# Re-ordering the attention phase of a four-layer fp32 transformer kernel on TensorE, and splitting a low part between two engines

## The chip, the cores and the metric
The kernel runs on one core of one Trainium2 chip. The metric is the device time of one execution in microseconds (us). TensorE is PE in the profile (PEld is its weight load), VectorE is DVE, ScalarE is ACT, GpSimd is POOL, SyncE is SP.

## The reference
Sixteen sequences of 256 tokens by 256 features go through four transformer layers, each conditioned by a vector per sequence. In every layer:

```
h = norm(x) * (1 + sc1) + sh1
x = x + gate1 * (softmax(q k^T / 4) v) @ Wo        # 16 heads of 16; layer 1 causal, layer 3 rotates q and k
h = norm(x) * (1 + sc2) + sh2
x = x + gate2 * act(h @ W1 + b1) @ W2              # W1: 256 -> 1024, gelu; layer 3: 256 -> 2048, a * silu(b)
```

All data are fp32. Layer 0 shares keys between heads (the weights are repeated, so the work is the same), layer 1 is causal, layer 3 has rotary positions, a root-mean-square norm and the gated hidden layer.

## The kernel before
**Tiles and steps.** A tile is one sequence in one layer, so there are 64. The work is a software pipeline over steps t: in a step, tile t+1 (`s.q`) gets its first norm and its queries, keys and values, tile t (`s.a`) its scores, softmax and outputs, tile t-1 (`s.r`) its output projection and second norm, and tile t-2 (`s.m`) its hidden layer (`up` and `down`, eight each). Eleven steps of each layer (44 in all) run in a hardware loop; the others are written out. In a loop, semaphores are compared with values held in registers. All five queues (PE, ACT, DVE, POOL, SP) are written out by hand in one order each, and wait for each other by semaphores. That order is what the change edits.

**Split products.** A product of two fp32 matrices is made of fp32r parts, a high part and a low part (value minus high part): high by high, low by high, high by low. `H2[0]` and `H2[1]` are the two parts of the second norm's result, the input of the `up` products. `project` issues six products of 256 columns per 128 outputs.

**The attention phase.** Scores are computed twice. First in the normal layout, from which DVE takes row maxima (`maximum`); then transposed with the maxima subtracted (`transposed_pair(p)`, L713, two heads in two halves of 64 rows), from which ACT takes the exponentials (L885) into a ring `PR` of 8 heads. `outputs(g)` (L738) multiplies four heads of `PR` by V in columns of 32. In front of the exponential of head h, ACT waits for `pe_pv` of outputs group h//4 - 2, which frees the ring:

```
at_least(ac, pe_pv, 4 * a_ + h // 4 - 1)
```

A transposed pair waits until the heads that used its PSUM banks four heads earlier are exponentiated. The first lines of each step's end on PE are: queries, pairs 0 and 1, maxima, keys, pairs 2 and 3, values half 0, outputs 0, pairs 4 and 5, outputs 1, second norm (`norm_2`, L592, four transposes), pairs 6 and 7, outputs 2, values half 1, outputs 3. In the causal layer each pair is followed by two mask products (L507).

**Second norm.** PE transposes TOK into a bank; DVE (`modulate_2`) writes HF (L1089, twice) and its high part H2h (L1095); POOL then writes the low part H2l (L1271). The next step begins on PE with `up(0)`, `up(1)`, which need both parts, then `outputs_to_tokens` (L602), `up(2)`, `down(0)`. `up(2)` writes the bank of `up(0)` and so waits for the activation of `up(0)` (`ac_g`, L861; in layer 3 `dv_g`, L966).

Of the kernel before, what the change touches and what calls it, by code (L numbers as in the profile page):

```python
# [21 lines left out]
F32 = mybir.dt.float32  # L22
# [52 lines left out]
NORM2_BANK = (0, 7)  # L75
# [9 lines left out]
def build(nc, a, out):  # L85
    ctx = ExitStack()
    with ctx:
# [52 lines left out]
        def bank(n, parts=2):  # L140
# [15 lines left out]
        dv_max, dv_rz, dv_on, dv_ot, dv_wo, dv_dn, dv_gh, dv_g, dv_swap, dv_rot, dv_rot2, dv_v, dv_o, dv_f2 = (  # L156
            sem("dv_" + x) for x in ("max", "rz", "on", "ot", "wo", "dn", "gh", "g", "swap", "rot", "rot2", "v", "o", "f2"))
# [321 lines left out]
        def _(pe):  # L479
# [23 lines left out]
            def body(s):  # L503
# [45 lines left out]

                def up(j):  # L550

                    m, dst = s.m, bank(3 - j % 2)
                    if j == 0:
                        weights(s.lm, "1", s.sm, *((0, 4, 2, 6) if s.lm == ROPE else (0, 2)))
                        pe.wait_ge(dv_h2, m + 1)
                        pe.wait_ge(po_h2, m + 1)
                        key_read(s)
                    elif j == 1:
                        at_least(pe, dv_v, s.nq)
                    elif s.lm == ROPE:  # L560
                        pe.wait_ge(dv_g, NJ * (m - NSEQ * ROPE) + j - 1)
                    else:
                        pe.wait_ge(ac_g, NJ * m + j - 1)
                    if j == NJ // 2:
                        weights(s.lm, "1", s.sm, *((1, 5, 3, 7) if s.lm == ROPE else (1, 3)))
                    last = project(dst[:, 0, :], cols(W1, j * P), H2)
                    if s.lm == ROPE:
                        last = project(dst[:, 1, :], cols(W1, DFF + j * P), H2)
                    last.then_inc(pe_up, 1)
# [57 lines left out]
                def norm_2():  # L627

                    if s.a is not None:
                        pe.wait_ge(ac_exp, H * s.a + last_user(ST_BANKS[rope][0:HB] + (NORM2_BANK[rope],), HB) + 1)  # L630
                    pe.wait_ge(dv_xn2, s.r + 1)
                    to_features(bank(NORM2_BANK[rope]), TOK).then_inc(pe_h2, 1)

# [88 lines left out]
                def outputs(g):  # L722
# [6 lines left out]
                    if g == 2:  # L729
                        at_least(pe, dv_dn, s.m_done)  # L730
                        if rope and s.r is not None:
                            pe.wait_ge(dv_f2, s.r + 1)
# [24 lines left out]
                up_if(0, 1)  # L757
# [39 lines left out]
                if scored:  # L797
                    transposed_pair(2)
                    transposed_pair(3)
                    values(0)  # L800
                    outputs(0)
                    transposed_pair(4)
                    transposed_pair(5)
                    outputs(1)
                    if s.r is not None:
                        norm_2()
                    transposed_pair(6)
                    transposed_pair(7)
                    outputs(2)
                    values(1)  # L810
# [10 lines left out]
        def _(ac):  # L821
# [84 lines left out]
            def modulate_1(s):  # L906
# [3 lines left out]
                at_least(ac, dv_h2, s.nr)  # L910
# [11 lines left out]
        def _(dv):  # L922
# [22 lines left out]
            def body(s):  # L945
# [136 lines left out]
                def modulate_2():  # L1082
# [12 lines left out]
                    nc.vector.tensor_copy(H2[0][:], HF[:]).then_inc(dv_h2, 1)  # L1095

# [17 lines left out]
                if s.lq == ROPE:  # L1114
# [7 lines left out]
                    rotate(s, pe_k, 3, GK, V_BK, V_BKR, 1)  # L1122
                    modulate_2()
                    evacuate(0)
                    values_out()
# [3 lines left out]
                else:  # L1129
                    split_q()  # L1130
                    split_k()
                    normalise_2()
                    modulate_2()
                    evacuate(0)
                    values_out()
# [60 lines left out]
        def _(po):  # L1196
# [40 lines left out]
            def body(s):  # L1237
# [30 lines left out]
                if s.r is not None:  # L1268
                    po.wait_ge(dv_f2, s.r + 1)
                    po.wait_ge(dv_h2, s.r + 1)  # L1270
                    nc.gpsimd.tensor_tensor(H2[1][:], HF[:], H2[0][:].bitcast(F32), ALU.subtract).then_inc(po_h2, 1)  # L1271
# [174 lines left out]
```

## Time and profile before

| | us |
|---|---|
| median of 3 runs | 2283.18 (2279.66 to 2284.66) |
| the profiled execution's own time | 2276.1 |
| its span in the trace | 2274.3 |
| PE busy | 2175.1 (96% of the span) |
| DVE busy | 1701.4 |
| ACT busy | 1252.4 |
| POOL busy | 1087.9 |

A line of the page's groups or of the timeline gives the source line, the engine, the operation, what it writes and reads, and how often. Matmuls are pipelined: one of 256 columns has a duration of 0.28 us, while the next starts 0.12 us after it, so starts are to be compared, not durations.

### The profile page before, as it was taken

To read this page: it belongs to the slowest core of one execution; us is meant where nothing else is said; L and a number is where in the kernel's file an instruction comes from. 1 tells how busy PE (TensorE), PEld (TensorE's weight loads), DVE (VectorE), ACT (ScalarE), POOL (GpSimd) and SP (SyncE) were. 2 spreads that over 40 slices of the span, in tenths; PEclk is the share of its full clock that TensorE was granted. 3 is DMA by queue.
4 is the path that set the end of the run, shared out by engine and by line. 5 is a ranking of instruction groups with operands and counts; after the bars stand their busy time and mean duration, and the time that the engine had idled before them with its cause. 6 is when DMAs were issued, how large, how long until landed. Compare 5 with 4: busy or idle time off the path is not lost.

```text
span 2274.3 us, 63435 instructions
## 1 busy us (share of the span) xinstructions
PE 2175.1 (96%) x20136; PEld 1824.5 (80%) x20136; DVE 1701.4 (75%) x4378; ACT 1252.4 (55%) x2620; POOL 1087.9 (48%) x1333
## 2 busy tenths in 40 slices
PE   5699999999999999999999999999999999999997
PEld 4578888888888888888878888888787878787877
DVE  3567777777777766776787777777888888888873
ACT  1366666666665555555676666666645444535341
POOL 1244554445544544454555444455554445444444
PEclk7699999999999999999999999999999999999998
DMA  6221222222221122112232222212221111111210
GB/s 230 89 72 64 63 69 70 71 64 77 89 91 63 58 70 72 60 59 92 90 99 64 70 74 65 63 63 80 83 78 66 59 63 60 62 64 58 68 58 15
DMA packets 164960, 166.12 MB, mean 73 GB/s; under 512 B 29328, under 2 KB 144400, under 8 KB 164848
## 3 DMA queue, kind: packets, MB, share of 16 engines
q1 hardware_dynamic: 164848, 164.69, 22.5%
q8 instruction: 63, 1.03, 0.2%
q14 instruction: 49, 0.40, 0.1%
HBM read 58.47 MB, written 4.39 MB: 28 GB/s over the span
## 4 chain that ended last, share of the span: by engine, by line
PE 86%; DVE 6%; issue 2%; SPq 1%; ACT 1%; POOL 1%; DMA 1%; POOLq 0%; ACTq 0%; DVEq 0%
PE B L483 36%; PE B L583 14%; PE B L738 10%; PE B L713 8%; PE B L530 7%; PE B L592 4%; PE B L602 2%; PE B L507 2%; DVE NEGM L959 2%; PE B L686 2%; SPq L1346 1%; ACT PR L885 1%; DVE G L966 0%; ACT G L855 0%; POOL GHl L1241 0%
## 5 line engine op out<-in xcount | busy, mean ns | idle before, releaser
L885 ACT ACTIVATE PR<-B 128x512 f32<-128x512 f32 (+1 forms) x1024 | 505.2, 570 | 277.2 <-PE B L713 186.6
L1241 POOL TENSOR_TENSOR GHl<-G,GHh 128x256 fp32r<-128x256 f32 x512 | 377.8, 738 | 472.7 <-ACT GHh L861 286.7
L959 DVE TENSOR_REDUCE NEGM<-B 128x2 f32<-128x512 f32 x768 | 484.6, 681 | 93.1 <-PE B L530 93.0
L483 PE MATMUL B<-H2h,W1h 128*128 128x256 f32 x1280 | 397.1, 310 | 3.1 <-issue 3.1
L483 PE MATMUL B<-H2h,W1l 128*128 128x256 f32 x1280 | 362.7, 283 | 0.0
L483 PE MATMUL B<-H2l,W1h 128*128 128x256 f32 x1280 | 362.1, 283 | 0.0
L861 ACT ACTIVATE G<-B,VEC 128x256 f32<-128x256 f32 x384 | 182.3, 475 | 291.7 <-PE B L483 291.7
L583 PE MATMUL B<-W2h,GHh 128*128 128x256 f32 x1024 | 296.4, 289 | 1.7 <-POOL GHl L1241 1.7
L583 PE MATMUL B<-W2l,GHh 128*128 128x256 f32 x1024 | 289.6, 283 | 0.0
L583 PE MATMUL B<-W2h,GHl 128*128 128x256 f32 x1024 | 288.9, 282 | 0.0
L483 PEld LDWEIGHTS B<-H2h,W1h 128*128 128x128 f32 x1280 | 243.8, 190 | 44.1 <-issue 26.0
L738 PE MATMUL B<-PR,V 128*32 128x256 f32 (+1 forms) x4096 | 262.6, 374 | 14.1 <-ACT PR L885 8.8
L1271 POOL TENSOR_TENSOR H2l<-HF,H2h 128x512 fp32r<-128x512 f32 x64 | 82.1, 1283 | 340.0 <-DVE H2h L1095 340.0
L483 PEld LDWEIGHTS B<-H2l,W1h 128*128 128x128 f32 x1280 | 244.8, 191 | 0.0
L483 PEld LDWEIGHTS B<-H2h,W1l 128*128 128x128 f32 x1280 | 243.9, 191 | 0.0
L713 PE MATMUL B<-QS,KS 64*128 64x256 f32 (+1 forms) x2048 | 226.2, 313 | 10.6 <-ACT PR L885 1.7
L713 PEld LDWEIGHTS B<-QS,KS 64*128 64x128 f32 x2048 | 151.1, 187 | 93.0 <-ACT PR L885 48.0
L530 PE MATMUL B<-KS,QS 48*128 48x256 f32 (+1 forms) x2048 | 199.1, 311 | 19.3 <-DMA KS<-KHL 11.7
L583 PEld LDWEIGHTS B<-W2h,GHh 128*128 128x128 f32 x1024 | 194.9, 190 | 10.4 <-DVE GHh L971 2.1
L956 DVE CUSTOM_DVE_ANT_0 B<-B,MASK 128x128 f32<-128x128 f32 (+1 forms) x512 | 165.6, 388 | 39.9 <-PE B L530 39.9
L583 PEld LDWEIGHTS B<-W2l,GHh 128*128 128x128 f32 x1024 | 195.3, 191 | 0.0
L583 PEld LDWEIGHTS B<-W2h,GHl 128*128 128x128 f32 x1024 | 195.3, 191 | 0.0
(149 smaller groups left out, 4737.4 us busy)
## 6 DMA issues: line engine op xcount, KB each, us to landing
QS<-QHL SPq DMA_DIRECT2D x768, 64.0 KB, 2.1
KS<-KHL SPq DMA_DIRECT2D x768, 64.0 KB, 2.1
GA<-gate_scratch SPq DMA_DIRECT2D x48, 256.0 KB, 3.2
GM<-gate_scratch SPq DMA_DIRECT2D x48, 256.0 KB, 3.4
RAW<-in_w SPq DMA_DIRECT2D x36, 256.0 KB, 3.2
CW<-in_cw SPq DMA_DIRECT2D x3, 1536.0 KB, 13.5
X<-in_x SPq DMA_DIRECT2D x2, 2048.0 KB, 10.3
QS<-MT SPq DMA_DIRECT2D x256, 4.0 KB
```

The lines of the kernel that those rows point to most:

```text
L483: last = nc.tensor.matmul(dst, w[i], x[j], start=(first_k and n == 0), stop=(last_k and n == 2))
L530: last = nc.tensor.matmul(bank(banks[h])[:, i, 0:keys], QS[b:b + STK, p, i * P:(i + 1) * P], KS[b:b + STK, p, 0:keys], start=True, stop=True)
L583: last = nc.tensor.matmul(bank(7)[:, i, :], GH[x][:, j % RING, i * P:(i + 1) * P], W2[y][:, j, :], start=(j == 0 and n == 0 and i == 0), s ...
L592: last = nc.tensor.transpose(dst[:, f, i * P:(i + 1) * P], src[:, i, f * P:(f + 1) * P], IDENT[:])
L713: last = nc.tensor.matmul(B[:, banks[h], k * T:k * T + T - first], KS[b:b + ROWS, p, k * P:(k + 1) * P], QS[b:b + ROWS, p, first:T], start ...
L738: last = nc.tensor.matmul(bank(6 + g // 2)[32 * j:32 * j + 32, g % 2, c], V[:, k, HV * h:HV * h + 32], PR[:, h % PRING, k, 0:n], start=(k ...
L861: last = nc.scalar.activation(dst[:, j % RING, :], bank(3 - j % 2)[:, 0, :], ACT.Gelu, bias=VEC[:, s.lm, V_B1 + j:V_B1 + j + 1])
L885: nc.scalar.activation(PR[:, h % PRING].rearrange("p k q -> p (k q)")[:, 0:n], src[:, 0:n], ACT.Exp, scale=SCALE).then_inc(ac_exp, 1)
L956: last = nc.vector.tensor_tensor_reduce(src[:, i, 0:keys], src[:, i, 0:keys], unmasked, -1.0, HIGHEST, ALU.add, ALU.min, NEGM[:, i, c:c + 1])
L959: last = nc.vector.tensor_reduce(NEGM[:, :, c], src, op=ALU.max, axis=AX.X, negate=True)
L1241: nc.gpsimd.tensor_tensor(GH[1][:, j % RING, :], G[:, j % RING, :], GH[0][:, j % RING, :].bitcast(F32), ALU.subtract).then_inc(po_gl, 1)
L1271: nc.gpsimd.tensor_tensor(H2[1][:], HF[:], H2[0][:].bitcast(F32), ALU.subtract).then_inc(po_h2, 1)
```

## The change
Seven edits, in the code's order:

- The bank of the second norm's transposes becomes 3 in layer 3 (it was 7); elsewhere it stays bank 0. `norm_2` there waits for the rotation of the keys, and `outputs(2)` no longer waits for `dv_f2`.
- The PE order of the attention phase: values half 0 comes in front of pairs 2 and 3, values half 1 in front of pairs 4 and 5, outputs 0 and 1 behind pairs 4 and 5, `norm_2` behind pairs 6 and 7 (in layer 3 behind outputs 2 as well).
- `up(0)` and `up(1)` become `first_ups`: first the products that read H2's high part for both, then those that read its low part for both.
- H2's low part is halved: DVE subtracts feature half 0 (`dv_h2lo`), POOL half 1.
- DVE evacuates the values (`values_out`) in front of `modulate_2`.

```diff
-NORM2_BANK = (0, 7)
+NORM2_BANK = (0, 3)
...
+                def first_ups():
+
+                    m = s.m
+                    weights(s.lm, "1", s.sm, *((0, 4, 2, 6) if s.lm == ROPE else (0, 2)))
+                    pe.wait_ge(dv_h2, m + 1)
+                    halves = [(0, 0), (1, DFF)] if s.lm == ROPE else [(0, 0)]
+                    for low in range(2):
+                        for j in range(2):
+                            dst = bank(3 - j)
+                            if low and j == 0:
+                                pe.wait_ge(dv_h2lo, m + 1)
+                                pe.wait_ge(po_h2, m + 1)
+                            elif j == 0:
+                                key_read(s)
+                            elif not low:
+                                at_least(pe, dv_v, s.nq)
+                            for half, c in halves:
+                                w = cols(W1, c + j * P)
+                                terms = [(0, k) for k in range(KD)] if low else [(i, k) for k in range(KD) for i in range(2)]
+                                for n, (i, k) in enumerate(terms):
+                                    last = nc.tensor.matmul(dst[:, half, :], w[i][:, k], H2[low][:, k],
+                                                            start=(n == 0 and not low and half == 0), stop=(n == KD - 1 and low == 1),
+                                                            skip_group_check=True)
+                            if low:
+                                last.then_inc(pe_up, 1)
...
                 def norm_2():
 
-                    if s.a is not None:
-                        pe.wait_ge(ac_exp, H * s.a + last_user(ST_BANKS[rope][0:HB] + (NORM2_BANK[rope],), HB) + 1)
+                    if rope:
+                        pe.wait_ge(dv_rot, 2 * (s.q - NSEQ * ROPE) + 2)
+                    elif s.a is not None:
+                        pe.wait_ge(ac_exp, H * s.a + last_user(ST_BANKS[0][0:HB] + (NORM2_BANK[0],), HB) + 1)
...
                     if g == 2:
                         at_least(pe, dv_dn, s.m_done)
-                        if rope and s.r is not None:
-                            pe.wait_ge(dv_f2, s.r + 1)
...
-                up_if(0, 1)
+                if s.m is not None:
+                    first_ups()
...
                 if scored:
+                    values(0)
                     transposed_pair(2)
                     transposed_pair(3)
-                    values(0)
-                    outputs(0)
+                    values(1)
                     transposed_pair(4)
                     transposed_pair(5)
+                    outputs(0)
                     outputs(1)
+                    transposed_pair(6)
+                    transposed_pair(7)
+                    if rope:
+                        outputs(2)
                     if s.r is not None:
                         norm_2()
-                    transposed_pair(6)
-                    transposed_pair(7)
-                    outputs(2)
-                    values(1)
+                    if not rope:
+                        outputs(2)
                     outputs(3)
...
                     nc.vector.tensor_copy(H2[0][:], HF[:]).then_inc(dv_h2, 1)
+                    dv.wait_ge(dv_h2, s.r + 1)
+                    nc.vector.tensor_tensor(H2[1][:, 0], HF[:, 0], H2[0][:, 0].bitcast(F32), ALU.subtract).then_inc(dv_h2lo, 1)
...
-                    nc.gpsimd.tensor_tensor(H2[1][:], HF[:], H2[0][:].bitcast(F32), ALU.subtract).then_inc(po_h2, 1)
+                    nc.gpsimd.tensor_tensor(H2[1][:, 1], HF[:, 1], H2[0][:, 1].bitcast(F32), ALU.subtract).then_inc(po_h2, 1)
```

## Rows read from the trace of the kernel before

**Rows 1.** Windows, a step each: us, busy PE, PEld, DVE, ACT, POOL; clock, DMA

```profile
1449.33:1480.97 31.64, 31.39 (x300) 26.17 (x296) 24.14 (x51) 20.30 (x43) 15.85 (x19) 1.00 0.22 67
1032.36:1064.89 32.53, 32.53 (x316) 27.19 (x312) 23.40 (x95) 19.32 (x45) 17.73 (x21) 1.00 0.27 86
1872.97:1911.55 38.58, 37.36 (x349) 32.05 (x345) 33.29 (x76) 17.52 (x34) 18.18 (x24) 1.00 0.20 62
```

**Rows 2.** Timeline of PE, layer 2, end of a step and start of the next

```profile
1469.32 0.74 PE L713 MATMUL B<-QS,KS 64*128 64x256 f32 x8
...
1471.86 1.13 PE L713 MATMUL B<-QS,KS 64*128 64x256 f32 x8
...
1473.81 1.07 PE L738 MATMUL B<-PR,V 128*32 128x256 f32 x16
1474.82 0.74 PE L713 MATMUL B<-QS,KS 64*128 64x256 f32 x8
...
1476.49 0.66 PE L592 MATMUL B<-IDENT,TOK 128*128 128x128 f32 x4
...
1477.64 0.50 PE L713 MATMUL B<-QS,KS 64*128 64x256 f32 x4
...
1479.08 0.38 PE L483 MATMUL B<-WQ0h,H1h 128*128 128x256 f32 x1
...
1479.97 1.07 PE L738 MATMUL B<-PR,V 128*32 128x256 f32 x16
1480.97 0.39 PE L483 MATMUL B<-H2h,W1h 128*128 128x256 f32 x1
...
1482.52 1.03 PE L602 MATMUL B<-IDENT,OR 128*128 128x128 f32 x8
1483.31 0.36 PE L483 MATMUL B<-H2h,W1h 128*128 128x256 f32 x1
```

**Rows 3.** Timeline of ACT over the same stretch of layer 2

```profile
1472.39 2.07 ACT L885 ACTIVATE PR<-B 128x512 f32<-128x512 f32 x4
...
1475.43 2.07 ACT L885 ACTIVATE PR<-B 128x512 f32<-128x512 f32 x4 [0.97 <-PE B L713]
...
1482.20 0.47 ACT L861 ACTIVATE G<-B,VEC 128x256 f32<-128x256 f32 x1 [0.94 <-PE B L483]
1482.57 0.47 ACT L861 ACTIVATE GHh<-B,VEC 128x256 fp32r<-128x256 f32 x1
```

**Rows 4.** Timeline of DVE over the same stretch of layer 2

```profile
1477.42 1.00 DVE L1089 TENSOR_SCALAR HF<-B,COND 128x256 f32<-128x256 f32 x2 [2.33 <-PE B L592]
1478.54 0.43 DVE L1095 CAST H2h<-HF 128x512 fp32r<-128x512 f32 x1
```

**Rows 5.** The page's costliest groups, the low part of the hidden layer

```profile
L1241 POOL TENSOR_TENSOR GHl<-G,GHh 128x256 fp32r<-128x256 f32 x512 | 377.8, 738 | 472.7 <-ACT GHh L861 286.7
```

**Rows 6.** One line's instructions (L258): ns min/median/max, first and last start

```profile
L258 DVE TENSOR_TENSOR W1l<-RAW,W1h x16: 659/682/1440, 55.8 to 1686.9; 128x512 fp32r<-128x512 f32 x16
```

**Rows 7.** Timeline of PE, causal layer 1

```profile
1055.36 0.44 PE L713 MATMUL B<-QS,KS 64*128 64x256 f32 x4
...
1057.47 0.86 PE L738 MATMUL B<-PR,V 128*32 128x256 f32 x16
...
1061.72 0.45 PE L713 MATMUL B<-QS,KS 64*128 64x256 f32 x4
```

**Rows 8.** Timeline of ACT, causal layer 1

```profile
1058.95 1.64 ACT L885 ACTIVATE PR<-B 128x384 f32<-128x384 f32 x4 [1.25 <-PE B L507]
...
1065.92 0.47 ACT L861 ACTIVATE G<-B,VEC 128x256 f32<-128x256 f32 x1 [1.04 <-PE B L483]
```

**Rows 9.** Timeline of PE, layer 3

```profile
1860.62 0.74 PE L713 MATMUL B<-QS,KS 64*128 64x256 f32 x8
...
1870.07 1.07 PE L738 MATMUL B<-PR,V 128*32 128x256 f32 x16 [0.71 <-ACT PR L885]
```

**Rows 10.** Timeline of DVE, layer 3

```profile
1875.37 0.48 DVE L966 SCALAR_TENSOR_TENSOR G<-B,VEC,G 128x256 f32<-128x256 f32 x1 [0.51 <-ACT G L855]
```

More of the change, by code:

```diff
@@ L155, in build @@
             sem("dv_" + x) for x in ("st1", "mv1", "xn1", "st2", "mv2", "xn2", "h1", "h2", "qh", "q", "kh", "k"))
-        dv_max, dv_rz, dv_on, dv_ot, dv_wo, dv_dn, dv_gh, dv_g, dv_swap, dv_rot, dv_rot2, dv_v, dv_o, dv_f2 = (
-            sem("dv_" + x) for x in ("max", "rz", "on", "ot", "wo", "dn", "gh", "g", "swap", "rot", "rot2", "v", "o", "f2"))
+        dv_max, dv_rz, dv_on, dv_ot, dv_wo, dv_dn, dv_gh, dv_g, dv_swap, dv_rot, dv_rot2, dv_v, dv_o, dv_f2, dv_h2lo = (
+            sem("dv_" + x) for x in ("max", "rz", "on", "ot", "wo", "dn", "gh", "g", "swap", "rot", "rot2", "v", "o", "f2", "h2lo"))
         po_t1, po_rs1, po_t2, po_rs2, po_h1, po_h2, po_gl, po_xb1, po_x1, po_xb2, po_x2, po_v, po_w, po_init, po_rot = (
@@ L548, in key_read @@
                         at_least(pe, dv_k, s.nq)
+                def first_ups():
[22 more added lines that the diff above has]
+                                last.then_inc(pe_up, 1)
                 def up(j):
                     m, dst = s.m, bank(3 - j % 2)
[L553 to L560, printed above, removed]
+                    if s.lm == ROPE:
                         pe.wait_ge(dv_g, NJ * (m - NSEQ * ROPE) + j - 1)
@@ L909, in modulate_1 @@
                     return
-                at_least(ac, dv_h2, s.nr)
+                at_least(ac, dv_h2lo, s.nr)
                 at_least(ac, po_h2, s.nr)
@@ L1122, in body @@
                     rotate(s, pe_k, 3, GK, V_BK, V_BKR, 1)
+                    values_out()
                     modulate_2()
                     evacuate(0)
-                    values_out()
                     evacuate(1)
@@ L1132, in body @@
                     normalise_2()
+                    values_out()
                     modulate_2()
                     evacuate(0)
-                    values_out()
                     evacuate(1)
```

## The prediction, on record before the run
> **What bounds the kernel now.** I read the windows first, one step each. PE is busy nearly all of a step (31.39 of 31.64 us in layer 2, 32.53 of 32.53 in the causal layer, 37.36 of 38.58 in layer 3) at full granted clock, and DVE, ACT and POOL are far from it [rows 1]. So a step is the sum of PE's starts, plus PE's waits. Durations overlap, therefore I read the timeline of PE by starts [rows 2]. Twelve first up products take 1482.52 - 1480.97 = 1.55 us: 12 x 0.12, and 0.10 to get going. Six V products between runs of other tile shapes take 1479.97 - 1479.08 = 0.89, against 6 x 0.12 = 0.72. Each change of shape (128 rows, pairs in 64 rows, outputs in 32 columns) thus costs about 0.17 to 0.18 us. The waits: the run of pairs 2 and 3 takes 1.13 where that of pairs 4 and 5 takes 0.74, and pair 7 starts only at 1477.64 [rows 2], 0.14 after ACT's group of exponentials 8 to 11 ends (1475.43 + 2.07 = 1477.50) [rows 3]. ACT's chain of exponentials therefore already touches PE's path. In layer 3 outputs 2 wait 0.71 at 1870.07 [rows 9].
>
> **What is removed.** In a layer without masks the new order has 10 shape changes from the queries to the next up where the old has 13: 3 x 0.17 = about 0.5 us a step. The wait of 0.39 in pairs 2 and 3 has half 0 of V as cover. In layer 3 the wait of 0.71 in outputs 2 loses its reason. The number of products is unchanged everywhere, so at PE alone I would book a gain of about 0.9 us a step, before new waits.
>
> The Trainium skill ("TensorEngine Tiling (Array Packing)", Key Properties) says that a change of tiling mode drains TensorE. By that, fewer changes are a gain; the 0.17 us agrees, and the sum needs nothing more from it.
>
> **What is added: the exponentials, layer 2 in a loop.** I schedule the new order by hand on the old clock, from the first pair at 1469.32, which nothing moves.
> - V half 0 comes ahead of pair 2, in the same shape as the keys before it: 6 x 0.12 = 0.71. Pair 2 goes from 1471.86 to 1472.57. ACT, idle by then, takes its exponential 4 at +0.61, the lag of pair 4 (1474.82) to exponential 8 (1475.43) [rows 2, 3]: 1473.18, where before it was at 1472.39.
> - Four exponentials take 2.07, spaced 0.49, 0.59 for one alone [rows 3]. Pair 4 needs heads 4 and 5: 1473.18 + 0.49 + 0.59 + 0.14 = 1474.41. Outputs 0 follow two pairs (0.67) later, at 1475.08, and end 1.07 later at 1476.15.
> - Exponential 8 overwrites the ring slot that outputs 0 read. Before, outputs 0 were over at 1474.88 and it went at 1475.43. Now it waits until about 1476.22: +0.79. Behind it in ACT's queue stand only exponentials and the table load (15 ends at 1480.2, in time for outputs 3 at 1480.33). Exponentials 8 to 11 end at 1478.29, pair 7 starts at 1478.43 instead of 1477.64.
> - Behind pair 7 (0.43) come the transposes at 1478.86. From their start to the end of H2h were 1478.97 - 1476.49 = 2.48 [rows 2, 4], and 0.14 to PE: 2.62. The high part is there for PE at 1481.48. Transposes and outputs 2 and 3 alone need 0.58 + 1.85 (1.01 each [rows 2] less the shape change between them) and are over at 1481.29. So the next step begins at 1481.48 instead of 1480.97: **+0.51**. The cover that H2h had (pairs 6 and 7, a half of V) is what the move took away.
>
> **What is added: the first ups.** `up(0)` now ends with the tenth product instead of the sixth: 4 x 0.12 = 0.48 later. Its activation ended 1482.57 + 0.47 - 1480.97 = 2.07 behind the step's start [rows 3, 2], with 0.14 it lets `up(2)` go at 2.21, and `up(2)` went at 2.34: 0.13 of room. So +0.35. What becomes late behind it is `down(0)`, whose low part follows the same activation; it moves along with `up(2)`.
>
> To it comes the halved low part. DVE's half starts 0.1 behind H2h and takes about 0.45 (an estimate: 256 columns, a little under the 0.48 of [rows 10]); POOL's takes 0.74 [rows 5]. If both run at once, POOL's half is there for PE 0.15 + 0.74 + 0.14 = 1.03 behind H2h, and the ninth product, the first to read it, is due at 0.14 + 0.10 + 8 x 0.12 = 1.20: hidden. If POOL has to wait for DVE, it is there at 0.1 + 0.45 + 0.03 + 0.74 + 0.14 = 1.46: 0.2 of stall. The trace has subtractions on DVE with two SBUF inputs that take 682 ns at the median and up to 1440 [rows 6], so such an instruction can be held up for as long as it runs. I take 0.2, and 0 as the lower bound. Together **+0.55**.
>
> The Trainium skill ("SBUF — State Buffer", Who interferes with whom) says that a DVE instruction with two SBUF inputs and a GpSimd instruction that reads SBUF exclude each other. By that the 0.2 is right; without it the sum would be 47 x 0.2 = about 9 us lower. The 1440 ns above agrees.
>
> `outputs_to_tokens` waits for DVE's two evacuations, which now come behind one more instruction; they end about 0.1 ahead of or behind its turn, inside the 0.55. POOL's copy of V, SP's loads of the stacks (released by pairs 3 and 7) and the moved `values_out` have more than 1 us until their readers, so I cost them at nothing.
>
> **The other steps.** Layer 0 has layer 2's order, so 22 loop steps: 22 x 1.06 = 23.3.
> - Causal, 11 loop steps, the same chain [rows 7, 8]: pair 2 at 1055.36 + 0.71 = 1056.07; pair, mask, pair, mask and V in 2.11, pair 4 at 1058.18; outputs 0 after two pairs with masks (1.40) at 1059.58 (before: 1057.47), over at 1060.44; exponential 8 at 1060.50 instead of 1058.95; number 11 over at 1062.14; pair 7 at 1062.28 instead of 1061.72; transposes 0.52 later; + 2.62 = 1065.42, where the window ends at 1064.89. +0.53, and +0.55: 11 x 1.08 = 11.9.
> - Layer 3, 11 loop steps, counted from pair 0 (1860.62 [rows 9]): exponential 4 at 3.86; pair 5 needs exponential 6, so 3.86 + 0.98 + 0.60 + 0.14 = 5.58; outputs 0 at 5.91, over at 6.98; exponential 11 over at 9.12; pair 7 at 9.27; outputs 2 at 9.70, transposes at 10.70, H2h for PE at 13.32, that is 1873.94 against 1872.97 [rows 1]: +0.97. The removed wait of 0.71 is thus paid back by one for H2h. `up(0)` has 24 - 4 = 20 products in front of its end instead of 12, 0.96 more; DVE's product ended at 1875.85 [rows 10], + 0.96 + 0.14 = 1876.95 against `up(2)` at 1872.97 + 24 x 0.12 + 0.10 + 0.79 = 1876.74: +0.2. 11 x 1.17 = 12.9.
> - The 19 scored steps outside the loops compare with constants: there the first activation comes 1065.92 - 1064.89 = 1.03 behind the step's start [rows 8, 1], not 1.23. With 0.2 off at each of two places I take 0.7: 13.3.
>
> Sum: 23.3 + 11.9 + 12.9 + 13.3 = 61 us on the profiled execution's 2276.1, so 2337. The median of the runs lies 7.1 above that execution: 2344.
>
> **The rivals.**
> - Forecast, slower by 32 to 80 us: the chain outputs 0, exponential 8, pair 7, transposes, H2h sets the step. Lower bound: no stall in the low part (-9), and waits in series shorter by 0.3 us a step than I read them (-19), so +32. Upper: each wait in a loop 0.3 longer, since `key_read` and others are now tested behind the wait for H2h: +80. Chance 0.84.
> - The exponentials hold PE back, but H2h doesn't, and the first ups cost only their 0.35 or less. Then a step is at +0.32 (1481.29 against 1480.97) + 0.15 to 0.35: 63 x 0.4 = +25, 2308. For it: PE and H2h differ by only 0.19 in layer 2. Against it: 0.97 in layer 3. Chance 0.06.
> - Faster: PE is the only bound. This needs exponential 8 not to wait on outputs 0, that is, outputs 0 over before 1475.43 + 0.3. Then -0.9 a step stays, +0.35 for the first ups: 62 x -0.55 = -34, 2249. For it: 96% busy. Against it: the code's wait, and a PE that is already held at pair 7. It decides when pair 4 starts before 1474.0. Chance 0.06.
> - No change: gain and waits cancel. It needs -0.5 us a step against my chain on both sides. 2283 within 4.6. Chance 0.04.
>
> **How the numbers follow.** Within 0.2% (4.6 us, what a measurement can tell) is the last rival; slower are the first two. The range 2308 to 2366 takes in the forecast's bounds (2315 and 2363) and the second rival's time. Slower 0.90, same 0.04, faster 0.06.
>
> **What would show it.** Layer 2's step at 32.7 instead of 31.64, layer 3's near 39.7, the causal one near 33.6; exponential 8 released by outputs 0 (L738), not by a pair; idle PE in front of pairs 6 and 7 and in front of the first up, released by H2h on DVE; ahead of `up(2)` a wait on ACT's activation; POOL's half of H2l starting behind DVE's. If pair 7 follows pair 6 without a gap, or PE finds H2h ready, I am wrong.

## The result, and the profile after

The changed kernel takes 2332.09 us (median of 4 runs, 2329.48 to 2337.9) against 2281.45 us for the kernel before (median of 4, 2279.66 to 2284.66): 1.0228 times as long, with a 95% interval of 1.0211 to 1.0244. The forecast was 2344 in a range of 2308 to 2366. The profiled execution took 2329.48 us against the 2276.1 on which the sum was made: +53.4, where the sum said +61. Runs of one kernel differ by up to 9 us, and some 6 of them can lie ahead of the first layer: of 96 products in the set-up (L360, the same in both), the last starts at 34.2 in the trace of the kernel before, where one takes 263 ns, and at 40.4 in that of experiment 10, where one takes 374.

The page of the changed kernel: the line of busy engines, the line of the chain that ended last, and one group of the costliest.

```profile
PE 2170.3 (93%) x20136; PEld 1833.4 (79%) x20136; DVE 1719.0 (74%) x4442; ACT 1249.2 (54%) x2620; POOL 1059.1 (46%) x1333
...
PE 81%; DVE 6%; ACT 4%; issue 4%; SPq 1%; DMA 1%; POOL 1%; ACTq 0%; DVEq 0%; POOLq 0%
...
L1266 POOL TENSOR_TENSOR GHl<-G,GHh 128x256 fp32r<-128x256 f32 x512 | 377.6, 738 | 458.9 <-ACT GHh L884 280.4
```

ACT's share of the chain was 1% in the kernel before, and PE's 86%. PE has as many products as before and is less busy in time, so all of the loss is idle PE. One step each of layer 2, of the causal layer 1 and of layer 3, windows of the changed kernel (columns as in [rows 1]):

```profile
1518.34:1550.95 32.61, 31.41 (x297) 26.35 (x297) 24.36 (x53) 20.24 (x43) 15.38 (x19) 1.00 0.20 65
889.18:922.79 33.61, 32.65 (x312) 27.56 (x313) 23.78 (x96) 18.47 (x43) 15.35 (x19) 1.00 0.20 63
1918.46:1957.96 39.50, 37.26 (x345) 32.07 (x345) 33.56 (x78) 17.38 (x34) 17.72 (x24) 1.00 0.18 60
```

Against [rows 1] the steps are 0.97, 1.08 and 0.92 us longer at the same granted clock of 1.00, and PE, which had 0.00 to 1.22 us of idle time in a step, has 0.96 to 2.24. The engines that got more to do (DVE in every layer) stay below the step's length (33.56 of 39.50 for DVE in layer 3 at most).

Timeline of PE in the changed kernel, layer 2, from the first pair of a step through the first ups of the next:

```profile
1538.85 0.74 PE L734 MATMUL B<-QS,KS 64*128 64x256 f32 x8
...
1542.08 0.74 PE L734 MATMUL B<-QS,KS 64*128 64x256 f32 x8
...
1543.86 0.76 PE L734 MATMUL B<-QS,KS 64*128 64x256 f32 x8
1544.55 1.93 PE L757 MATMUL B<-PR,V 128*32 128x256 f32 x32
1546.92 0.50 PE L734 MATMUL B<-QS,KS 64*128 64x256 f32 x4 [0.43 <-ACT PR L908]
1547.90 0.50 PE L734 MATMUL B<-QS,KS 64*128 64x256 f32 x4 [0.48 <-ACT PR L908]
1548.33 0.66 PE L611 MATMUL B<-IDENT,TOK 128*128 128x128 f32 x4
1548.92 1.93 PE L757 MATMUL B<-PR,V 128*32 128x256 f32 x32
1550.95 0.38 PE L570 MATMUL B<-H2h,W1h 128*128 128x256 f32 x1
...
1552.01 0.71 PE L570 MATMUL B<-H2l,W1h 128*128 128x256 f32 x4
1552.56 1.06 PE L621 MATMUL B<-IDENT,OR 128*128 128x128 f32 x8
1553.62 0.39 PE L483 MATMUL B<-H2h,W1h 128*128 128x256 f32 x1
...
1554.54 0.36 PE L602 MATMUL B<-W2h,GHh 128*128 128x256 f32 x1
```

Timeline of ACT over the same stretch:

```profile
1542.62 2.07 ACT L908 ACTIVATE PR<-B 128x512 f32<-128x512 f32 x4 [0.76 <-PE B L734]
1545.69 4.03 ACT L908 ACTIVATE PR<-B 128x512 f32<-128x512 f32 x8 [0.99 <-PE B L757]
...
1553.10 0.47 ACT L884 ACTIVATE GHh<-B,VEC 128x256 fp32r<-128x256 f32 x1
```

The line to see is ACT's second one. In [rows 3] the exponentials 8 to 11 waited for a pair (`<-PE B L713`). Here number 8 waits for outputs 0 (`<-PE B L757`), which are the first half of PE's row x32 at 1544.55 and are over about 1.07 later. Counted from pair 0, exponential 8 starts at 6.84 (before: 1475.43 - 1469.32 = 6.11), and from there all is late. Pair 6 waits 0.43, pair 7 waits 0.48 and starts at 9.05 (before 8.32), the transposes of the second norm follow at 9.48, and the next step's first up comes at 12.10 where it came at 11.65: +0.45.

Timeline of PE in layer 3 of the changed kernel, the same stretch:

```profile
1944.81 0.74 PE L734 MATMUL B<-QS,KS 64*128 64x256 f32 x8
...
1954.01 0.50 PE L734 MATMUL B<-QS,KS 64*128 64x256 f32 x4 [0.48 <-ACT PR L908]
...
1955.44 0.66 PE L611 MATMUL B<-IDENT,TOK 128*128 128x128 f32 x4
1956.02 1.07 PE L757 MATMUL B<-PR,V 128*32 128x256 f32 x16
1957.96 0.38 PE L570 MATMUL B<-H2h,W1h 128*128 128x256 f32 x1 [0.86 <-DVE H2h L1118]
```

Here the transposes come last but for outputs 3, and PE stands idle for 0.86 us on the high part of the norm. That takes the place of the wait of 0.71 in [rows 9], which is gone.

The low part of the second norm, timelines of DVE and POOL in layer 2, and the page's view by line (ns min/median/max):

```profile
1549.27 0.99 DVE L1112 TENSOR_SCALAR HF<-B,COND 128x256 f32<-128x256 f32 x2 [4.05 <-PE B L611]
1550.39 0.43 DVE L1118 CAST H2h<-HF 128x512 fp32r<-128x512 f32 x1
1550.85 0.43 DVE L1120 TENSOR_TENSOR H2l<-HF,H2h 128x256 fp32r<-128x256 f32 x1
```
```profile
1550.97 0.90 POOL L1296 TENSOR_TENSOR H2l<-HF,H2h 128x256 fp32r<-128x256 f32 x1 [9.29 <-DVE H2h L1118]
...
1553.65 1.46 POOL L1266 TENSOR_TENSOR GHl<-G,GHh 128x256 fp32r<-128x256 f32 x2 [1.23 <-ACT GHh L884]
```
```profile
L1296 POOL TENSOR_TENSOR H2l<-HF,H2h x64: 894/906/919, 131.2 to 2301.4; 128x256 fp32r<-128x256 f32 x64
```
```profile
L1120 DVE TENSOR_TENSOR H2l<-HF,H2h x64: 424/426/429, 131.1 to 2301.3; 128x256 fp32r<-128x256 f32 x64
```

POOL's half takes 906 ns at the median (894 to 919 in all 64 steps), where the same operation on the same shape takes 738 elsewhere (L1266). DVE's takes 426 and begins 0.12 us earlier in this step.

**A step taken apart.** For the experiments a step is cut in two: from its first up to the queries ("first part") and from the queries to the next first up ("attention"). Both are differences of starts in PE's timeline, for one step inside each loop, in us (other steps in the middle of a loop differ from it by 0.04 or less):

```
              layer 0          causal           layer 2          layer 3
before        18.33 + 13.17    18.42 + 14.11    18.47 + 13.18    24.69 + 13.89
after         18.87 + 13.60    18.94 + 14.67    19.02 + 13.63    24.83 + 14.67
difference     0.54 +  0.43     0.52 +  0.56     0.55 +  0.45     0.14 +  0.78
```

### The profile page after: what moved, and what is told of

It is laid out like the page before. It is cut to its first block, busy times and chain, and to the rows that moved or that the text cites. A ratio compares the mean times of both kernels' runs of the same rounds, so it can differ in the third digit from the quotient of the medians.

```text
span 2327.7 us, 63529 instructions
## 1 busy us (share of the span) xinstructions
PE 2170.3 (93%) x20136; PEld 1833.4 (79%) x20136; DVE 1719.0 (74%) x4442; ACT 1249.2 (54%) x2620; POOL 1059.1 (46%) x1333
## 4 chain that ended last, share of the span: by engine, by line
PE 81%; DVE 6%; ACT 4%; issue 4%; SPq 1%; DMA 1%; POOL 1%; ACTq 0%; DVEq 0%; POOLq 0%
PE B L483 30%; PE B L602 15%; PE B L734 8%; PE B L530 7%; PE B L757 6%; PE B L570 6%; PE B L611 4%; ACT PR L908 4%; PE B L621 2%; PE B L507 2%; PE B L707 2%; DVE NEGM L982 2%; SPq L1371 1%; DVE HF L1112 1%; DVE H2h L1118 1%
## 5 line engine op out<-in xcount | busy, mean ns | idle before, releaser
L1266 POOL TENSOR_TENSOR GHl<-G,GHh 128x256 fp32r<-128x256 f32 x512 | 377.6, 738 | 458.9 <-ACT GHh L884 280.4
L483 PE MATMUL B<-H2h,W1h 128*128 128x256 f32 x960 | 300.7, 313 | 0.5 <-DVE G L989 0.2
L1296 POOL TENSOR_TENSOR H2l<-HF,H2h 128x256 fp32r<-128x256 f32 x64 | 57.9, 905 | 495.8 <-DVE H2h L1118 495.8
L734 PE MATMUL B<-QS,KS 64*128 64x256 f32 (+1 forms) x2048 | 218.3, 310 | 59.8 <-ACT PR L908 52.6
L483 PE MATMUL B<-H2h,W1l 128*128 128x256 f32 x960 | 271.6, 283 | 0.0
L483 PE MATMUL B<-H2l,W1h 128*128 128x256 f32 x960 | 271.2, 283 | 0.0
L1112 DVE TENSOR_SCALAR HF<-B,COND 128x256 f32<-128x256 f32 x128 | 63.7, 540 | 254.9 <-PE B L611 254.9
L757 PE MATMUL B<-PR,V 128*32 128x256 f32 (+1 forms) x4096 | 239.3, 371 | 0.4 <-ACT PR L908 0.4
L483 PEld LDWEIGHTS B<-H2h,W1h 128*128 128x128 f32 x960 | 182.0, 190 | 28.7 <-ACT GHh L884 8.0
L530 PEld LDWEIGHTS B<-KS,QS 48*128 48x128 f32 x2048 | 140.8, 187 | 63.8 <-issue 19.9
## 6 DMA issues: line engine op xcount, KB each, us to landing
X<-in_x SPq DMA_DIRECT2D x2, 2048.0 KB, 10.3
```

The lines of the kernel that those rows point to most:

```text
L483: last = nc.tensor.matmul(dst, w[i], x[j], start=(first_k and n == 0), stop=(last_k and n == 2))
L530: last = nc.tensor.matmul(bank(banks[h])[:, i, 0:keys], QS[b:b + STK, p, i * P:(i + 1) * P], KS[b:b + STK, p, 0:keys], start=True, stop=True)
L734: last = nc.tensor.matmul(B[:, banks[h], k * T:k * T + T - first], KS[b:b + ROWS, p, k * P:(k + 1) * P], QS[b:b + ROWS, p, first:T], start ...
L757: last = nc.tensor.matmul(bank(6 + g // 2)[32 * j:32 * j + 32, g % 2, c], V[:, k, HV * h:HV * h + 32], PR[:, h % PRING, k, 0:n], start=(k ...
L1266: nc.gpsimd.tensor_tensor(GH[1][:, j % RING, :], G[:, j % RING, :], GH[0][:, j % RING, :].bitcast(F32), ALU.subtract).then_inc(po_gl, 1)
```

## The experiments

Unless a ratio is said to be to something else, it is to the kernel before, run beside on the same chip, with its 95% interval.

**1. The first ups and the halved low part alone.** The kernel before, with `first_ups()` and both subtractions as in the change; order, banks and `values_out` stay as they were.

```diff
-                up_if(0, 1)
+                if s.m is not None:
+                    first_ups()
...
+                    dv.wait_ge(dv_h2, s.r + 1)
+                    nc.vector.tensor_tensor(H2[1][:, 0], HF[:, 0], H2[0][:, 0].bitcast(F32), ALU.subtract).then_inc(dv_h2lo, 1)
...
-                    nc.gpsimd.tensor_tensor(H2[1][:], HF[:], H2[0][:].bitcast(F32), ALU.subtract).then_inc(po_h2, 1)
+                    nc.gpsimd.tensor_tensor(H2[1][:, 1], HF[:, 1], H2[0][:, 1].bitcast(F32), ALU.subtract).then_inc(po_h2, 1)
```

> The kernel before with the low-part edits alone (first ups in two passes, low part halved between DVE and POOL); the order of the attention phase, the banks and values_out stay. Theory A (up(0) ends four products later, up(2) waits for its activation): a step in a loop of layers 0 to 2 is 0.35 us longer, one outside 0.15, one of layer 3 0.2; about +16 us in all, 2297. All of it between the step's start and up(2); the attention phase is unchanged. Rival B (the 0.54 us that the changed kernel loses there comes from the late high part and from POOL's half alone): here the parts are ready early, so within 5 us of the kernel before.

Measured: 2298.86 us, 1.0073 [1.0045, 1.0101]. The attention of layer 2 stays at 13.20, the first part grows from 18.47 to 18.92. So these edits reach only the first part, as the forecast's chain wants it, and cost 0.45 of the 0.55 us there, where 0.35 was expected.

**2. The order alone.** The kernel before with the new order, banks and place of `values_out`, but the old `up(0)` and `up(1)`, and the whole low part on POOL.

```diff
-NORM2_BANK = (0, 7)
+NORM2_BANK = (0, 3)
...
                 if scored:
+                    values(0)
                     transposed_pair(2)
                     transposed_pair(3)
-                    values(0)
-                    outputs(0)
+                    values(1)
                     transposed_pair(4)
                     transposed_pair(5)
+                    outputs(0)
                     outputs(1)
-                    if s.r is not None:
-                        norm_2()
                     transposed_pair(6)
                     transposed_pair(7)
...
+                        norm_2()
+                    if not rope:
+                        outputs(2)
                     outputs(3)
```

> The changed kernel with the old ups and the whole low part on POOL: the new order alone. Theory A (the high part of H2 is the last thing to come, and the low part 1.44 us behind it is hidden only by the two passes): the first up goes 1.44 us later than in the changed kernel, 0.54 us of it is won back before up(2); about +0.9 us a step in layers 0 to 2 and +1.3 in layer 3, 2395 us. Rival B (the exponentials alone hold PE back and the low part has cover): at or below the changed kernel's 2332, since the 0.54 us in the first ups goes away.

Measured: 2406.68 us, 1.0548 [1.0521, 1.0575]. Timelines of PE and of POOL, layer 2:

```profile
1472.43 0.38 PE L483 MATMUL B<-H2h,W1h 128*128 128x256 f32 x1 [1.62 <-POOL H2l L1274]
```
```profile
1470.93 1.26 POOL L1274 TENSOR_TENSOR H2l<-HF,H2h 128x512 fp32r<-128x512 f32 x1 [9.29 <-DVE H2h L1098]
```

With the late norm the old first ups wait for POOL's whole subtraction: 1470.93 + 1.26 + 0.14 = 1472.33, and the first of them starts at 1472.43. The time is 12 us above the 2395 expected. The attention takes 15.15 instead of 13.18. Two things follow. The new order alone is far worse than the change as a whole. And the edits of the low part, two passes and halving together, are a repair of it: with them the order costs 0.45 us in layer 2 instead of 1.97, and their own price of 0.55 is on top. How much of the repair each of the two gives in the new order, no run shows.

**3. Outputs 0 back ahead of pairs 4 and 5.** The changed kernel, one line moved.

```diff
                     values(1)
+                    outputs(0)
                     transposed_pair(4)
                     transposed_pair(5)
-                    outputs(0)
                     outputs(1)
```

> The changed kernel with outputs 0 moved back in front of pairs 4 and 5 (behind V half 1). Theory A (exponential 8 waits for the ring slot that outputs 0 read): exponential 8 is released by pair 4, about 0.45 us earlier, pair 7 and the high part of H2 as well, and a step is about 0.45 us shorter although it has one shape change more; about -27 us against the changed kernel, 2305. Rival C (V half 0 ahead of pair 2 delays all exponentials and is the whole cause) and rival D (the second norm's place): exponentials 8 to 15 come no earlier for PE, 2332 within 5 us.

Measured: 2300.97 us, 1.0090 [1.0064, 1.0117], so 31 us less than the changed kernel, and near experiment 1, which has the low-part edits and none of the order. Timeline of ACT, layer 2:

```profile
1399.65 4.03 ACT L908 ACTIVATE PR<-B 128x512 f32<-128x512 f32 x8 [0.59 <-PE B L734]
```

Exponential 8 is released by a pair again, 6.43 behind pair 0 (which starts at 1393.22), and the attention of layer 2 is back at 13.22, that of layer 3 at 14.05. The first part keeps its 19.00. This one line holds nearly the whole of what the order costs. That it does not fall below 13.18, although two shape changes fewer are made than before, is the rest of the lateness: both halves of V now stand in front of outputs 0, which start 4.82 behind pair 0 (1398.04 in PE's timeline) instead of 4.49.

**4. The norm back ahead of pairs 6 and 7.** The changed kernel, layers 0 to 2.

```diff
                     outputs(1)
+                    if s.r is not None and not rope:
+                        norm_2()
                     transposed_pair(6)
                     transposed_pair(7)
...
```

> The changed kernel with the second norm's transposes in front of pairs 6 and 7 in layers 0 to 2 (layer 3 as changed). Theory A (the exponentials are late by 0.8 us whatever the norm does): the transposes fill the wait at pair 6, but outputs 3 wait for exponential 15; the attention phase is 0.1 us shorter, the low part's wait in the first ups goes: -0.2 us in 47 steps, about 2323. Rival D (the norm's place behind the last pairs is the cause): the attention phase falls by the 0.4 us it grew or more, 2311 or lower.

Measured: 2317.93 us, 1.0157 [1.0129, 1.0185], 14 less than the changed kernel (16 by the two ratios), between the two expectations. The attention of layer 2 goes from 13.63 to 13.44, that of the causal layer from 14.67 to 14.07. Timelines of ACT and of PE, layer 2, where pair 0 starts at 1528.67:

```profile
1535.51 4.03 ACT L910 ACTIVATE PR<-B 128x512 f32<-128x512 f32 x8 [1.00 <-PE B L757]
```
```profile
1539.59 1.07 PE L757 MATMUL B<-PR,V 128*32 128x256 f32 x16 [0.37 <-ACT PR L910]
```

The exponentials are as late as in the changed kernel (6.84 behind pair 0). With the high part early enough, PE meets the next wait of the same chain: outputs 3 wait 0.37 for exponential 15. So in layer 2 the late ring is the root, and the norm's place decides only which of its ends PE feels. In the causal layer, whose exponentials take 1.64 us for four instead of 2.07, [rows 3, 8], the norm's place is enough: put back, its attention is 0.04 below the kernel before. But outputs 0 put back, with the norm left late, also take most of the loss away there (14.23 in experiment 3, against 14.67 and 14.11). So the loss in the causal layer needs both moves, and neither alone carries it.

**5 to 7. Filling without delay.** Three variants of the kernel before that take the idea of the change (V products as cover) and leave outputs 0 and the norm where they were. Number 5 puts three of the six products of half 0 ahead of pair 2 (`values` takes the k halves to issue as a second argument); number 6 puts half 1 ahead of outputs 2; number 7 has both.

```diff
+                    values(0, (0,))
                     transposed_pair(2)
                     transposed_pair(3)
-                    values(0)
+                    values(0, (1,))
                     outputs(0)
...
                     transposed_pair(7)
+                    values(1)
                     outputs(2)
-                    values(1)
                     outputs(3)
```

> The kernel before with one edit: the first three of the six products of V half 0 go ahead of pairs 2 and 3, the other three stay behind them. Theory A (what a filling is worth is the wait that it covers, as long as ACT's exponentials don't move back): the wait of 0.39 us at pair 3 goes and nothing behind it is late; -0.36 us in the 31 steps of layers 0 and 2, nothing in the causal layer, which has no such wait, and nothing in layer 3, where outputs 2 wait for DVE: about -11 us, ratio 0.995. Rival C (any V product ahead of pair 2 pushes the exponentials back): a step is as long as before or longer, ratio 1.000 or more.

> The kernel before with one edit: V half 1 ahead of outputs 2 instead of between outputs 2 and 3. Theory A: one shape change less in every step (-0.1 to -0.3 us), and in layer 3 the 0.9 us of V lie in the wait of 0.7 us that outputs 2 have for the second norm: about -0.7 us a step there. Together about -20 us, ratio 0.991. Rival: layer 3's wait moves to the first up (the low part of H2 comes 0.9 us ahead of it now), and the exponentials bind outputs 3; ratio 0.998 to 1.000.

> Both edits of the two kernels above. Theory A: they add up, since one covers a wait at pair 3 and the other one at outputs 2: -0.45 us a step in layers 0 and 2, -0.3 in the causal layer, -0.75 in layer 3, together about -31 us, ratio 0.986. Rival: the exponentials bind in both, so that the second edit gives nothing in layers 0 and 2: about -20 us, ratio 0.991.

Measured: 2267.64 us, 0.9941 [0.9926, 0.9956]; 2259.86 us, 0.9902 [0.9886, 0.9917]; 2253.27 us, 0.9872 [0.9856, 0.9888]. Number 5, timeline of PE in layer 2, the first pair of the step and pairs 2 and 3:

```profile
1371.47 0.74 PE L715 MATMUL B<-QS,KS 64*128 64x256 f32 x8
...
1374.35 0.78 PE L715 MATMUL B<-QS,KS 64*128 64x256 f32 x8
```

Pairs 2 and 3 take 0.78 where they took 1.13 in [rows 2]: the wait is covered. Exponential 4 now starts at 3.42 behind pair 0 instead of 3.07, but number 8, which outputs 0 don't hold up, starts at 5.76 instead of 6.11: nothing is paid for it. The attention falls from 13.18 to 12.84. In number 6 half 1 joins the outputs 2 and 3 into one run, which saves a shape change (13.18 to 13.05 in layer 2, 14.11 to 13.82 in the causal layer), and in layer 3 it covers the wait of [rows 9] (13.89 to 13.25). Number 7 has 31.15 us a step in layer 2.

**8. DVE's half of the low part later.** The changed kernel, with DVE's subtraction behind `evacuate(0)`, so that POOL's starts first.

```diff
                     evacuate(0)
+                    low_2()
                     evacuate(1)
```

> The changed kernel with DVE's half of the low part behind its first evacuation (a copy out of PSUM) instead of in front of it, so that POOL's half no longer starts beside it. Theory P (the two subtractions, each with two SBUF inputs, hold each other up): POOL's half falls from 0.906 us to the 0.738 us of the same shape in the hidden layer, and DVE's half, which now starts while POOL's still runs, grows from 0.426 us. The low part is complete about 0.15 us later, so the time is about 2338 us. Rival Q (POOL's half is long for another reason, its place behind a wait for instance): 0.906 and 0.426 us stay.

Measured: 2335.8 us, 1.0236 [1.0221, 1.0252]: the time is that of the changed kernel within the intervals. Timelines of POOL and DVE in one step, and POOL's instructions by line:

```profile
1559.51 0.73 POOL L1303 TENSOR_TENSOR H2l<-HF,H2h 128x256 fp32r<-128x256 f32 x1 [9.29 <-DVE H2h L1118]
```
```profile
1560.19 0.81 POOL L1308 COPY V<-VT 128x512 f32<-128x512 f32 x1
```
```profile
1559.87 0.65 DVE L1125 TENSOR_TENSOR H2l<-HF,H2h 128x256 fp32r<-128x256 f32 x1
```
```profile
L1303 POOL TENSOR_TENSOR H2l<-HF,H2h x64: 729/735/911, 137.9 to 2311.1; 128x256 fp32r<-128x256 f32 x64
```

POOL's half is back at 735 ns, and it is DVE's that grew, from 426 to 650. The engine that comes second pays. POOL's next instruction, the copy of V, then comes second behind DVE's and pays too: 0.81 us, where it takes 0.61 in the changed kernel.

**9. The two passes alone.** As experiment 1, but the whole low part stays on POOL (the ninth product waits for `po_h2` only).

```diff
                             if low and j == 0:
-                                pe.wait_ge(dv_h2lo, m + 1)
                                 pe.wait_ge(po_h2, m + 1)
```

> The kernel before with the first ups in two passes alone; the low part stays whole on POOL, DVE does nothing more. Theory A (four products more ahead of the end of up(0), and nothing else): a step is 0.45 us longer in the loops of layers 0 to 2, as in the kernel with all low-part edits, 0.14 in layer 3; +18 us. Rival H (DVE's subtraction, which puts its evacuations 0.4 us later, has a share in it): less than +12 us.

Measured: 2299.28 us, 1.0074 [1.0049, 1.0099], the same as experiment 1 with its 1.0073. In the old order, halving the low part has no share in the time; the two passes have all of it. Timelines of PE and POOL, layer 2:

```profile
1368.25 0.39 PE L569 MATMUL B<-H2h,W1h 128*128 128x256 f32 x1
...
1370.85 0.38 PE L483 MATMUL B<-H2h,W1h 128*128 128x256 f32 x1
...
1371.75 0.36 PE L601 MATMUL B<-W2h,GHh 128*128 128x256 f32 x1
```
```profile
1370.87 1.46 POOL L1260 TENSOR_TENSOR GHl<-G,GHh 128x256 fp32r<-128x256 f32 x2 [1.78 <-ACT GHh L880]
```

`up(2)` starts 2.60 behind the step's start, where it was 1483.31 - 1480.97 = 2.34 [rows 2], and `down(0)` at 3.50. That is POOL's time: 1370.87 + 0.73 + 0.14 = 1371.74. The same two in the kernel before, where `down(0)` did not wait (3.13):

```profile
1483.12 1.46 POOL L1241 TENSOR_TENSOR GHl<-G,GHh 128x256 fp32r<-128x256 f32 x2 [1.30 <-ACT GHh L861]
```
```profile
1484.10 0.28 PE L583 MATMUL B<-W2h,GHh 128*128 128x256 f32 x1
```

**10. Outputs 0 late, in the old kernel.** The kernel before with outputs 0 behind pairs 4 and 5 and nothing else.

```diff
                     values(0)
-                    outputs(0)
                     transposed_pair(4)
                     transposed_pair(5)
+                    outputs(0)
                     outputs(1)
```

> The kernel before with one edit: outputs 0 behind pairs 4 and 5 instead of in front of them; V, the second norm and the first ups stay. Theory A (the ring): exponential 8 waits for outputs 0, pair 7 starts 0.7 us later and outputs 3 wait for exponential 15; +0.7 us a step in the 31 steps of layers 0 and 2, -0.1 in the causal layer (whose exponentials are shorter, and one shape change goes), nothing in layer 3, whose outputs 2 wait for DVE until then; about +20 us. Rival G (the exponentials have room; what counts is the shape change saved): -0.15 us a step, -9 us.

Measured: 2296.32 us, 1.0059 [1.0036, 1.0082], slower as expected, by about 14.6 us instead of 20. Timelines of ACT and PE, layer 2, where pair 0 starts at 1387.53:

```profile
1394.38 4.03 ACT L885 ACTIVATE PR<-B 128x512 f32<-128x512 f32 x8 [1.71 <-PE B L738]
```
```profile
1392.81 0.50 PE L713 MATMUL B<-QS,KS 64*128 64x256 f32 x4 [0.28 <-DVE KHL L1183]
```

The sum over the layers hides different answers. In layer 2 the attention grows by 0.73, in layer 0 by 0.20, in layer 3 by nothing (13.88), and in the causal layer it falls by 0.12. In layer 2 a wait joins that I had not counted: pair 5, earlier now, waits 0.28 for DVE's split of the keys, and outputs 0 behind it are later still (exponential 8 at 6.85, in layer 0 at 6.30). In the causal layer the short exponentials leave room and only the saved shape change is left. In the trace the eleven loop steps of layer 2 are 8.0 us longer together, those of layer 0 2.1, those of the causal layer 1.4 shorter; most of the rest of the 14.6 lies in steps outside the loops. So outputs 0 behind pairs 4 and 5 are no loss in themselves; they are one where exponential 8 then waits for them, and in the changed kernel two halves of V stand in front of them as well.

**11. An order of its own for the causal layer.** Number 7, with no V products ahead of pair 2 there, and outputs 0 and 1 in one run.

```diff
+                if scored and s.la == CAUSAL:
+                    transposed_pair(2)
+                    transposed_pair(3)
+                    values(0)
+                    outputs(0)
+                    outputs(1)
+                    transposed_pair(4)
+                    transposed_pair(5)
...
+                    transposed_pair(6)
+                    transposed_pair(7)
+                    values(1)
+                    outputs(2)
+                    outputs(3)
```

> The kernel with both fillings, and in the causal layer an order of its own: pairs 2, 3, V half 0, outputs 0 and 1, pairs 4, 5, norm, pairs 6, 7, V half 1, outputs 2 and 3. Its exponentials take 0.37 us each instead of 0.48, so outputs 0 and 1 can stand side by side ahead of pair 4 without a wait: one shape change less, -0.2 us in 16 steps, -3 us; ratio 0.986 to the kernel before. Rival: a wait for exponential 7 in front of outputs 1 eats it: no difference from the kernel with both fillings (0.987).

Measured: 2250.12 us, 0.9868 [0.9847, 0.9889]. Windows of the causal step, first of number 7, then of this one:

```profile
865.21:897.43 32.22, 32.22 (x317) 27.30 (x313) 23.35 (x94) 18.40 (x43) 15.80 (x19) 1.00 0.20 66
```
```profile
862.81:894.75 31.94, 31.94 (x316) 27.45 (x313) 23.33 (x94) 18.41 (x43) 15.81 (x19) 1.00 0.22 66
```

The step is 0.28 us shorter; over the kernel that is about 3 us, which the ratios of the two don't tell apart. Numbers 7 and 11 are the versions to keep: 1.3% below the kernel before. Against the changed kernel, which did not run beside them, number 7 is about 3.4% lower (2253.27 / 2332.09 = 0.966).

## Why the prediction was right, and where its sizes were off

**The mechanism.** It went step by step as written. In layer 2, counted from pair 0, predicted and measured: exponential 4 at 3.86 and 3.77, exponential 8 at 6.90 and 6.84, pair 7 at 9.11 and 9.05, transposes at 9.54 and 9.48, the next first up at 12.16 and 12.10. From the transposes to the up are 2.62 in both. The whole chain is 0.06 to 0.09 early because exponential 4 is, and so the +0.51 measures +0.45. Experiment 3 shows the cause and not only the order of events: one line back, and the +0.45 is +0.04. That the norm's output, and not the exponentials, comes last is shown by the 0.86 us in front of layer 3's first up, by 0.52 in front of the causal layer's (at 922.79), and by experiment 2, where the input of the first ups comes later still and PE with it.

**The term of the shape changes.** I booked three changes at 0.17, 0.5 us. In layer 2 the waits inside the attention were 0.39 + 0.33 = 0.72 before (pairs 2 and 3, pairs 6 and 7) and are 0.20 + 0.50 + 0.75 + 0.16 = 1.61 now (pair 4, pair 6, pair 7, first up), each a block's length less what it takes undisturbed (0.67 for two pairs, 1.87 for two outputs). That is +0.89 for a growth of 0.45, so the changes gave 0.44, 0.15 each. The gain was there as forecast and the waits ate it twice over.

**The first ups.** +0.55 was the right sum of wrong parts. The two passes alone cost 0.45 (experiment 9) and not 0.35; the low part costs about 0.1 and not 0.2. What failed is the sentence that `down(0)` "moves along with `up(2)`". In experiment 9 `up(2)` moved by 0.26, less than my 0.35, because it starts 0.05 behind the end of ACT's activation (1553.10 + 0.47 against 1553.62), where I had taken 0.14. But POOL's low part of the same activation moved by the full 0.47 (2.62 behind the step's start instead of 2.15), and `down(0)` had only about 0.11 of room to it (1483.12 in the trace of before, + 0.73 + 0.14 = 1483.99, against 1484.10). So `down(0)` moved by 0.37, and inside it the rest was lost: its second product starts 0.20 behind the first, where it was 0.12 in the kernel before. I had followed the first reader of the late result to its end and taken the second on trust.

**The low part.** It cost about 0.08 to 0.1, between my bounds of 0 and 0.2: in the changed kernel the first ups take 1.62 (1550.95 to 1552.56, with rounding), in experiments 1 and 9 1.54. I had put POOL's start behind DVE's end. POOL's record starts 0.12 behind DVE's start and is 0.17 longer than alone, so the half is there at 1550.97 + 0.90 + 0.14 = 1552.01, 1.19 behind the end of H2h and not 1.46. That is the moment at which the ninth product was due: it comes on time, and what is lost is that the one behind it starts 0.20 later instead of 0.12.

**The layers.** A step in the middle of a loop costs 0.96 in layer 0 and 0.97 to 1.00 in layer 2 (predicted 1.06), 1.09 in the causal one (1.08), 0.93 in layer 3 (1.17). From the start of the first to the end of the last of its eleven steps each loop is longer by 10.3 (layer 0), 11.8 (causal), 10.6 (layer 2) and 10.1 (layer 3), as steps at a loop's ends cost less: 42.8 against 48.1. Layer 3 is the largest miss, 2.8 us: pair 7 comes at 9.20 (9.27 predicted), from the transposes to the up are 2.52 instead of 2.62, and the first part grows by 0.14 instead of 0.20. The steps outside the loops and the ends of the kernel took 53.4 - 42.8 = 10.6 against 13.3; I had taken 0.7 each as a round figure. Together that is the 8.0 us between 61.4 (the terms of my sum, given as 61) and 53.4. The rest of the distance to 2344 is the addition of 7.1 for the median: the changed kernel's median lies 2.6 above its profiled execution.

**The rivals.** That the exponentials hold PE back but the high part doesn't is refuted in layer 3 (0.86 of idle time in front of the first up) and in the causal layer (0.52), and close in layer 2, where the up follows only 0.16 late: there it would have cost 0.29 instead of 0.45. The faster rival wanted pair 4 ahead of the equivalent of 1474.0, 4.68 behind pair 0; it starts at 5.01. Its mechanism is real, as numbers 5 to 7 show: cover gains its wait when nothing is pushed back for it.

## What to carry to other kernels

Filling in front of a wait is worth the wait, not the filling's length. Half 0 of V is 0.71 us and stood in front of a wait of 0.39: the other 0.3 made all that stands behind it on PE later, and exponential 4 came 0.70 later. Three products did the same work, and nothing was paid for it.

Where a ring ties two engines, look up which instruction frees the slot and count from there to the slot's next writer; moving the freeing instruction is moving the writer, unless the writer has room (the causal layer in experiment 10). Moving what produces an input (the norm) closer to the reader of that input, here towards the end of a step, takes the cover off its whole chain, here 2.62 us long, and that has to be laid against what is left behind it.

When a result comes later, follow each of its readers, on every engine, to the first that has no room.

## What the runs showed of the hardware

**Two subtractions at once.** On DVE and POOL, both with two SBUF inputs, the one that starts second is slowed and the first is not: POOL 738 to 906 ns when it starts 0.12 behind DVE, DVE 426 to 650 ns when it starts 0.36 behind POOL. The overlap with the first one's run was 1551.28 - 1550.97 = 0.31 us in one case and 1560.24 - 1559.87 = 0.37 in the other, and the losses were 0.17 and 0.22. The copy of V in experiment 8, which has one SBUF input, had 1560.52 - 1560.19 = 0.33 of overlap and lost 0.20. The trace of the kernel before has a longer case:

```profile
615.90 1.28 POOL L1227 TENSOR_TENSOR X<-X,GA 128x512 f32<-128x512 f32 x1
```
```profile
616.31 1.41 DVE L258 TENSOR_TENSOR W1l<-RAW,W1h 128x512 fp32r<-128x512 f32 x1
```

The overlap is 617.18 - 616.31 = 0.87, and DVE loses 1.41 - 0.68 = 0.73 [rows 6]. So the loss isn't a share of the overlap: in all four cases it is the overlap less 0.13 to 0.15. The second one behaves as if it stood still until about 0.14 ahead of the recorded end of the first. I had counted on all or nothing, and on the whole of the first one's record. The Trainium skill ("SBUF — State Buffer", Who interferes with whom) speaks of an exclusive lock on a shared pair of ports. The traces agree that the second is held up for all of the first one's run but its last 0.14; what happens in that last part, no run here tells.

**The price of a shape change.** It is 0.15 us on average over the three that were saved, not one number: between V products and pairs I read 0.17 to 0.18, while a run of outputs alone takes 1.00 and two in one run 1.87 (1372.94 to 1374.81 in experiment 7, layer 2), so joining two runs of outputs is worth 0.13.
